# VectorE's loop over the thirteen middle images, written out: a convolution and pooling kernel on one core

## The reference

```
def _L0_conv_ref(x, W, bias):                    # x is already group-normalised
    gs = spatial_descriptor(x, 5)                # 25 channels: sum over channels of x * x shifted
    gs = gs / sqrt(sum(gs * gs) + 1e-6)
    out = einsum('bchw,oc->bohw', concatenate([x, gs]), W) + bias
    return relu(out)

x = x + _L0_conv_ref(_gn(x), L0_conv_W, L0_conv_bias)         # layer 0: the first stage
x = x + _L1_conv_ref(_gn(x), L1_conv_w1, ..., L1_conv_b2)     # layer 1: the second stage
```

## Time and profile before

| | |
|---|---|
| median of 3 runs | 4066.7 us (4065.01 to 4067.97) |
| the profiled execution's own time | 4064.64 us |
| its span, from first to last instruction | 4062.7 us |
| PE busy | 3398.5 us (84%) |
| DVE busy | 3302.9 us (81%) |
| POOL busy | 2043.7 us (50%) |
| ACT busy | 1970.4 us (49%) |
| first stage | from the start to about 2460 us |
| second stage, with the sorting | from there to the end |

### The profile page before, as it was taken

How to read it: one execution, slowest core, us unless ns; L and a number is a source line. 1 busy time by engine, 2 the same in 40 slices (tenths; PEclk the granted TensorE clock), 3 DMA queues, 4 the chain that set the end, 5 groups by cost and what they waited for, 6 DMA issues and landing times.

```text
span 4062.7 us, 83954 instructions
## 1 busy us (share of the span) xinstructions
PE 3398.5 (84%) x28232; PEld 1929.0 (47%) x28233; DVE 3302.9 (81%) x3619; ACT 1970.4 (49%) x3219; POOL 2043.7 (50%) x1564
## 2 busy tenths in 40 slices
PE   5999999999999999999999995455666667876775
PEld 3665665665666666566566664222222223332222
DVE  6777777777777777777777666999999999999997
ACT  4454544554544545445455530334444444654466
POOL 3555555555555555555555542344444553444543
PEclk9999999999999999999999996777888888998887
DMA  5454544544544545545445335464565666864466
GB/s 195 166 186 168 180 174 163 190 165 162 192 163 166 190 162 176 180 162 180 175 173 182 124 109 113 187 249 167 225 244 231 246 254 266 329 273 155 187 255 240
DMA packets 251672, 782.36 MB, mean 193 GB/s; under 512 B 97433, under 2 KB 97433, under 8 KB 229273
## 3 DMA queue, kind: packets, MB, share of 16 engines
q1 hardware_dynamic: 219600, 417.47, 29.5%
q0 software_dynamic: 31568, 358.89, 22.6%
HBM read 421.55 MB, written 409.08 MB: 204 GB/s over the span
## 4 chain that ended last, share of the span: by engine, by line
PE 62%; DVE 23%; issue 7%; ACT 4%; POOL 1%; DVEq 1%; DMA 1%; ACTq 1%; SPq 0%; POOLq 0%
DVE arena L1041 20%; PE psum L1198 15%; PE psum L1221 10%; PE psum L1222 10%; PE psum L1223 10%; PE psum L1401 6%; PE psum L1399 4%; PE psum L1245 3%; ACT psum L661 3%; PE psum L1280 2%; PE psum L1259 1%; DVE bnx L735 1%; PE psum L1367 1%; DVE bny L797 1%; PE psum L1270 1%
## 5 line engine op out<-in xcount | busy, mean ns | idle before, releaser
L1041 DVE TENSOR_TENSOR arena<-arena 128x2048 f32<-128x2048 f32 (+8 forms) x635 | 1454.8, 2320 | 62.9 <-DMA arena<-wide_planes,arena 13.8
L437 POOL TENSOR_TENSOR arena<-arena 128x512 f16<-128x512 f32 x512 | 617.8, 1208 | 1043.8 <-ACT arena L580 1043.5
L1399 PE MATMUL psum<-arena 128*128 128x512 f32 x896 | 534.2, 681 | 466.3 <-issue 329.5
L578 ACT ACTIVATE arena<-arena,gbias,grstd 128x512 f32 (+1 forms) x512 | 413.7, 808 | 760.7 <-PE psum L1223 677.9
L1221 PE MATMUL psum<-arena 128*128 128x512 f16 x2048 | 777.1, 379 | 1.0 <-ACT arena L592 1.0
L1198 PE MATMUL psum<-arena 128*128 128x256 f16 (+1 forms) x6344 | 728.3, 273 | 59.0 <-DVE arena L785 43.5
L1222 PE MATMUL psum<-arena 128*128 128x512 f16 x2048 | 776.7, 379 | 0.0
L1223 PE MATMUL psum<-arena 128*128 128x512 f16 x2048 | 776.3, 379 | 0.0
L1198 PEld LDWEIGHTS psum<-arena 128*128 128x128 f16 x6344 | 599.1, 100 | 146.1 <-DVE arena L785 46.0
L446 POOL TENSOR_TENSOR arena<-arena 128x512 f32 (+1 forms) x512 | 640.1, 1271 | 55.4 <-ACT arena L592 46.7
L675 ACT ACTIVATE arena<-psum 128x512 f32<-128x512 f32 x536 | 314.5, 598 | 694.8 <-PE psum L1401 684.2
(11 more groups left out here) (151 smaller groups left out, 2999.3 us busy)
## 6 DMA issues: line engine op xcount, KB each, us to landing
arena<-in_x SPq DMA_DIRECT2D x64, 2048.0 KB, 9.9
wide_planes<-arena SPq DMA_DIRECT2D x128, 1024.0 KB, 5.7
y_planes<-arena SPq DMA_DIRECT2D x64, 2048.0 KB, 10.3
arena<-arena SPq DMA_DIRECT2D x1536, 8.0 KB, 1.8
arena<-wide_planes,arena POOLq DMA_INDIRECT x69, 11.7
arena<-plane_records,arena POOLq DMA_INDIRECT x67, 7.7
arena<-y_planes,arena POOLq DMA_INDIRECT x67, 9.7
out<-arena POOLq DMA_INDIRECT x67, 9.1
```

The lines of the kernel that those rows point to most:

```text
L437: pool.tensor_tensor(gl[:, ct, slot], g32[:, ct % 2, :], gh[:, ct, slot], ALU.subtract).then_inc(s_gl, 1)
L578: act.activation(g32[:, ct % 2, :], piece, ACT.Identity, bias=gbias[:, ct:ct + 1], scale=grstd[:, ct:ct + 1])
L1041: ins = dve.tensor_tensor(dst, a, b, ALU.max)
L1399: pe.matmul(dst, diag[:, s, 0, :], small[:, s, b * ROWS:(b + 1) * ROWS, 1:W + 1], start=False, stop=False, skip_group_check=True)
```

## The change

One line differs. The loop on DVE's stream over images 1 to 13 becomes a Python loop, so that its body is written out thirteen times with the image number as a constant. No other engine's stream is touched.

```diff
             masks_of(0, 0, [[]] * PAIRS)
             image(0, first=True)
-            with dve.Fori(1, B - 2) as i:
+            for i in range(1, B - 2):
                 image(i)
             image(B - 2, left=1)
             image(B - 1, left=0)
```

## The result

| | median of the runs | range |
|---|---|---|
| before | 4065.86 us (4 runs) | 4059.35 to 4067.97 |
| after | 3995.18 us (4 runs) | 3993.63 to 3998.57 |
| ratio | 0.983 | 95% interval 0.9813 to 0.9847 |

The change takes 71 us away. The prediction was 4000 us with a range of 3988 to 4014. The profiled execution took 3993.63 us with a span of 3991.7, against 4062.7 before.

A forecast was written before the change was run, and what follows sets the result against it. PE bounds the first stage but stalls at DVE's twelve branches back; removing them saves 66.8 us, other terms 0. The profiled 4064.64 becomes 3997.8 us, with 4000 forecast for the median, range 3988 to 4014.

The forecast's parts named there:

- The step that carries the sum: PE's images 2 to 13: 1815.99 us, against 145.6 each without DVE's branch, less 2.0 for PE's own; 66.8 us saved.
- The reading of what bounds PE there: After DVE's branch back, PE idles 3.41 us for mask 0, then runs two blocks at clock 0.50, 5.30 us against 2.78.
- Who takes DVE's place: At image boundaries: ACT's and POOL's branches cost PE nothing; SP's, with 1.6 us to spare, was costed at nothing.
- Rival (b): SP's branch at image boundaries eats part of the gain: 2 us an image, 24 in all, 4024 us; chance 7%.
- PE's own branch: PE's branch back into image 8, where it sits 1.99 us, was expected to stay.
- The register form at DVE: Register instructions leaving DVE's first-stage stream: value 0, bounds 0.5 us to either side, from images 1 and 14.
- The code behind the loop: DVE's second-stage code moves in memory; two idle stretches may change: value 0, bounds 12.1 us to either side.
- The packet of the earlier trace: A packet of instructions (0.02 MB) between DVE's branch and next mask, read as its stream being brought in again.
- (a), the image boundary: The stall belongs to the image boundary, colliding with the 1 MB store; only 0.8 us goes, 4065.9 us; chance 3%.
- (c), straight code that waits for itself: DVE stalls once in each of images 1 to 14, costing 78 us against 66.8 saved: 4078 us; chance 3%.
- (d), the clock: Without pauses PE's granted clock falls in the first stage; 3% lower eats the whole gain, 4068 us; chance 2%.

The follow-up runs named there:

- others_written: Against the kernel before: first-stage loops of SP, POOL, ACT and PE written out, DVE's loop kept; 4042.81 us, ratio 0.9949.

## Why the prediction was right

**The size.** The step that carries the sum, 1815.99 - 12 x 145.6 - 2.0 = 66.8 us, measured 66.3 on the same calendar. The images that took no branch back had been the right yardstick. The reading of what bounds PE there, the wait for mask 0 and the slow clock behind it, is borne out too: both are gone.

**Who takes DVE's place.** Nobody, as said. ACT's and POOL's branches stay hidden. SP's, which no row of before covered, showed nothing either: between 210 and 2090 us PE has no wait for the regrouped descriptor. Rival (b) is out.

**PE's own branch stays** at 2.0 us, against the earlier trace rows.

**The register form at DVE** was valued at 0 with bounds of 0.5 us. That was a little too narrow: the two kernels without branches differ by some 3 us in the first stage. The images compared then (1 and 14) each differ from a full middle image, so they bounded it too tightly. The prediction also counts exactly twelve waits of DVE that no semaphore explains; there were 23 short ones besides, before L806. They are there again with the register form (8.8 us in 26 waits), where PE has no wait for the masks, so they don't touch the sum.

**The code behind the loop.** Valued at 0 with bounds of 12.1 us to either side; DVE's stalls in the second stage came out 4.0 us shorter and the stage 4.7. This is most of what lies between the 3997.8 summed for the profiled execution and the 3993.6 measured, and no row of before could have told it. The reason given, that the code moves, is not borne out. DVE's stream in others_written is that of the kernel before, instruction for instruction, and yet its waits put down to issue in the second stage (2440 us to the end) come to 6.6 us and not 12.1:

```profile
DVE arena L1041 <- issue: 6.6, 2, 4.7
```

From image 15 to the end that kernel is 5.2 us shorter than before, and the kernel after 4.2. So a stall at one of these branches changes without any change of DVE's stream, and it is not shown that the 4.7 us come from the change. That it stayed small beside the 66.3 was in part luck, since the bounds allowed 12.1.

**Whose packets they are.** The packet of the earlier trace rows that the prediction took for DVE's code is on q8, and q8's count follows PE's stream: 228 packets in each run that leaves that as it is, 221 where PE's first-stage loop is written out. What a change of DVE's stream moves is q14's count (276 before, 221 after). The same stretch before, 350 to 357 us, has two packets there, so the reading holds with another line:

```profile
q14 instruction: 2, 0.02, 0.6%
```

**The other rivals.** (a), the image boundary, is out by the run after itself, which has the boundaries and the store and no stall. (c), straight code that waits for itself, is out: no wait put down to issue before the masks in 3377 straight instructions. (d), the clock, is out: 1.00 over 1880 us.

The Trainium skill's rule for taken branches ("Runtime: NRT & Kernel Launch", section "Instruction fetch mechanics"), that a target outside the blocks held is fetched before execution goes on, agrees with the runs: 12 stalls with the far branch forward, none with the near one back. What the same section of the Trainium skill says of running straight on, that crossing a block's end is mostly hidden, agrees as well: DVE in the kernel after has no wait put down to issue from 210 to 2090 us. The Trainium skill's other figure ("Advanced Engine Details and Errata", section "Control Flow Timing"), about 108 ns for a compare-and-branch, is not what the traces have: 53 ns for the near branch, 63 for the far one, and behind the far one 5.7 us to the next instruction.

One number of the description ahead of the prediction is off: a written-out body has not some 240 instructions but about 206 (453 + 2223 = 2676 for thirteen). Nothing rests on it.

## What to carry to other kernels

Count the engine's idle stretches that no semaphore explains and compare the count with the turns of its loops; where they match, price a branch back by the calendar of the engine that waits, since idle time and slow clock are both in it. Look at which engine bounds the stage before writing a loop out: here VectorE's was worth 66 us although VectorE was not the bound, since its stall of 4.8 us was longer than the 1.3 us to spare. Where an engine is the bound itself, its register instructions cost too: 0.5 us an image on TensorE, 7.4 us in the second stage on VectorE.

## What the runs showed of the hardware that was not expected

- The price of a far branch depends on the transfers beside it: 2.0 us of idle at 21.9% busy transfer engines, 4.8 us at 99.4%.
- A branch forward over 600 instructions makes nearly the stall of a branch back over 453 (4.6 us of idle, 50.7 / 11, against 4.8), and a branch back of three instructions nothing that can be seen. Where between three and 453 the price begins, no run shows.
- Writing the loop out made DVE's stream longer by 2223 instructions and the instruction traffic smaller, 276 to 221 packets on q14. The register form without branches has 246, so 25 of the 55 packets go with the register instructions and 30 with the twelve branches, 2.5 for each.
- An idle stretch of PE of 3.4 us halved the granted clock (0.50) for the blocks behind it, 5.30 us for work of 2.78; one of 2.0 us and those of 0.85 us did not. In between the length does not decide: behind 3.13 us (two images in a turn) and 2.44 us (far branch forward, image 3) the two blocks took 2.79 us, behind 2.40 us (far branch forward, image 12) 4.46.
